# GpSimd's sum of the exponentials takes in key block 4, and the second queries' denominators are multiplied together one step later

## What is computed

```python
scores = jnp.einsum('bsnh,btnh->bnst', k, q) / math.sqrt(HEAD_SIZE)
ones = jnp.ones_like(scores)
scores = jnp.triu(scores) + -10000.0 * jnp.tril(ones, k=-1)
attn = jax.nn.softmax(scores, axis=2)
out = jnp.einsum('bnkq,bknh->bqnh', attn, v)
```

## Time and profile before

| | before |
|---|---|
| median of 3 runs | 1672.31 us (1671.54 to 1673.26) |
| profiled execution, its own time | 1674.67 us |
| its span, first to last instruction | 1672.8 us |
| PE busy | 1574.5 us, 94% of the span |
| DVE busy | 957.4 us, 57% |
| ACT busy | 742.1 us, 44% |
| POOL busy | 601.9 us, 36% |
| mean granted PE clock | 0.977 |

### The profile page before, as it was taken

The page is one execution under the profiler, slowest core; times in us unless marked ns, Lnnn a source line. Parts: engine busy times, 40 slices in busy tenths (PEclk is TensorE's granted clock), DMA queues, the critical chain, the costliest instruction groups (busy, mean ns, idle before and its releaser), DMA issues.

```text
span 1672.8 us, 24916 instructions
## 1 busy us (share of the span) xinstructions
PE 1574.5 (94%) x9630; PEld 671.1 (40%) x9632; DVE 957.4 (57%) x1784; ACT 742.1 (44%) x1206; POOL 601.9 (36%) x808
## 2 busy tenths in 40 slices
PE   5899999999999999999997699999999999999997
PEld 2334333443443434334432234444444444444443
DVE  5667766778766777667777333563534343434344
ACT  5346555566555665556655433232222222222221
POOL 4344654567456755655666630020000000000000
PEclk8899999999999999999988889999999999999998
DMA  5212111222220233012215631121101010101000
GB/s 183 90 50 52 50 28 51 66 73 80 79 61 24 79 85 95 25 40 79 85 47 159 213 109 45 52 100 32 51 26 51 25 51 26 51 25 51 0 26 26
DMA packets 59398, 106.25 MB, mean 64 GB/s; under 512 B 11408, under 2 KB 11408, under 8 KB 59024
## 3 DMA queue, kind: packets, MB, share of 16 engines
q1 hardware_dynamic: 59280, 104.66, 20.3%
HBM read 54.02 MB, written 25.17 MB: 47 GB/s over the span
## 4 chain that ended last, share of the span: by engine, by line
PE 70%; DVE 11%; POOL 8%; issue 4%; ACT 4%; DMA 1%; SPq 1%; DVEq 0%; ACTq 0%; POOLq 0%
PE ps L865 25%; PE ps L786 15%; PE ps L882 12%; PE ps L849 9%; DVE mcol L1105 6%; POOL pt L1311 4%; PE ps L823 4%; ACT pt L968 2%; PE ps L799 2%; PE ps L807 1%; DVE st L995 1%; PE ps L753 1%; POOL rs L1236 1%; SPq L665 1%; POOL pt L1302 1%
## 5 line engine op out<-in xcount | busy, mean ns | idle before, releaser
L968 ACT ACTIVATE pt<-ps,nrm 128x512 f32<-128x512 f32 (+1 forms) x640 | 362.1, 645 | 339.4 <-PE ps L823 310.2
L865 PE MATMUL ps<-x2in,gu 128*128 128x512 f16 x2048 | 463.9, 380 | 0.0
L1105 DVE TENSOR_REDUCE mcol<-ps 128x1 f32<-128x512 f32 (+3 forms) x768 | 369.5, 546 | 81.5 <-PE ps L807 53.8
L865 PEld LDWEIGHTS ps<-x2in,gu 128*128 128x128 f16 x2048 | 200.7, 98 | 240.8 <-issue 1.9
L1233 POOL TENSOR_SCALAR rs<-mv 128x1 f32<-128x1 f32 x120 | 24.9, 207 | 665.6 <-DVE mv L999 660.1
L1180 DVE SCALAR_TENSOR_TENSOR hf<-ps,usc,sg 128x512 f32<-128x512 f32 x128 | 96.1, 751 | 265.2 <-PE ps L865 252.6
L1311 POOL TENSOR_TENSOR pt<-pt 128x1024 f32<-128x1024 f32 x96 | 227.5, 2390 | 2.9 <-ACT pt L968 2.4
L984 ACT ACTIVATE hh<-hf 128x512 f16<-128x512 f32 x128 | 80.7, 631 | 261.7 <-DVE hf L1180 248.1
L882 PE MATMUL ps<-wd,hh 128*128 128x512 f16 x512 | 194.0, 379 | 0.0
L882 PE MATMUL ps<-wd,hl 128*128 128x512 f16 x512 | 194.0, 379 | 0.0
L823 PE MATMUL ps<-qpack,kpack 98*128 98x512 f16 (+3 forms) x768 | 169.2, 337 | 23.1 <-DVE mcol L1105 16.5
(11 more groups left out here) (116 smaller groups left out, 1618.0 us busy)
## 6 DMA issues: line engine op xcount, KB each, us to landing
qpack<-stage SPq DMA_DIRECT2D x192, 64.0 KB, 2.0
kpack<-stage SPq DMA_DIRECT2D x192, 64.0 KB, 2.0
xr<-in_x SPq DMA_DIRECT2D x32, 256.0 KB, 2.8
x1d<-xr SPq DMA_DIRECT2D x32, 256.0 KB, 2.4
x2d<-x2s SPq DMA_DIRECT2D x32, 256.0 KB, 2.0
x2in<-x2d SPq DMA_DIRECT2D x8, 1024.0 KB, 5.6
x1in<-x1d SPq DMA_DIRECT2D x8, 1024.0 KB, 5.8
out_x<-yy SPq DMA_DIRECT2D x32, 256.0 KB, 2.0
```

The lines of the kernel that those rows point to most:

```text
L865: mm = pe.matmul(bk, GU[:, c, m, i * 128:(i + 1) * 128], x2in[:, 1 - k, :, p, c, :], start=p == 0 and c == 0, stop=p == 1 and c == 3)
L968: act.activation(Pt[:, PBUF[step], h, off:512], ps[:, BANK[job], off:512], ACT.Exp, scale=esc).then_inc(s_ex, 1)
L1105: mm = dve.tensor_reduce(mcol[:, n % 2, col:col + 1], ps[:, BANK["max", n, i, h], at:at + w], AX.X, ALU.max)
```

## The change

POOL's sum takes in block 4 as well: two more additions of 128x1024 elements in step 8 of each group, the first ahead of the selects of block 5, the second behind them (in groups 14 and 15 both ahead). The den job of block 4 is gone. The den jobs of the sum and of block 5 leave step 9 and stand, with that of blocks 6 and 7, in step 0 of the next group, ahead of num. Bank 7 therefore stays in `RING` until step 0, where the sum's den job now opens the accumulation. Two waits come with it: the exponentials of block 6 wait for POOL's addition of block 4, which read the same buffer, and those of step 0 of the next group wait for block 5's den job. In groups 14 and 15 the den jobs of step 0 stand behind the scores of that step.

```diff
--- before.py
+++ after.py
@@ -150,12 +150,12 @@
 
     if step is None:
         return []
-    summed = step[1] == 1 and step[2] < 4
-    out = [] if summed else [("den",) + step]
+    of, j, kb = step
+    out = [("den", of, j, k) for k in ([kb] if j == 0 else [0, 5, 6] if last(j, kb) else [])]
     out.append(("num",) + step)
-    if summed and step[2] > 0:
-        out += [("sum",) + step + (h,) for h in (0, 2) if h == 0 or s != 7 or n >= NG - 2]
-    return out + [("den", n, 1, 0)] * (s == NS - 1)
+    if j == 1 and 0 < kb < 5:
+        out += [("sum",) + step + (h,) for h in (0, 2) if h == 0 or s not in (7, 8) or n >= NG - 2]
+    return out
 
 
 def order_of_jobs():
@@ -216,7 +216,7 @@
             plan += [("score", n, j, kb, h) for h in range(4)]
             if n < NG - 2 and pend is not None and last(*pend[1:]):
                 plan += [("invert",) + pend[:2], ("normalise",) + pend[:2]]
-            if s == 7 and n < NG - 2:
+            if s in (7, 8) and n < NG - 2:
                 add(("sum",) + pend + (2,))
             if s == NS - EARLY and n + 1 < NG:
                 plan += [("mjoin", n + 1), ("mturn", n + 1)]
@@ -237,7 +237,7 @@
             pend = (n, j, kb)
         if n + 2 < NG:
             add(("packs", n + 2))
-    plan += [("den",) + pend, ("num",) + pend, ("invert",) + pend[:2], ("normalise",) + pend[:2]]
+    plan += products_of(pend, NG, 0) + [("invert",) + pend[:2], ("normalise",) + pend[:2]]
     tail = [with_dev(job) for s in range(12) for job in rows.get(NS * NG + s, [])]
     started = max(job[1] for job in plan if job[0] == "woproj") + 1
     left = list(range(started, NT))
@@ -339,7 +339,7 @@
     elif kind == "step":
         if 5 in RING:
             RING.remove(5)
-        if 7 in RING and job[2] == 8:
+        if 7 in RING and job[2] == 0:
             RING.remove(7)
         if job[2] not in projections(job[1]) and FREE == [5]:
             RING.append(5)
@@ -350,7 +350,7 @@
             RING.append(7)
         continue
     elif kind == "den":
-        if job[2:] in ((0, 0), (1, 4)):
+        if job[3] == 0:
             FREE = [5]
             take(job, 7)
         continue
@@ -381,7 +381,8 @@
 
 
 
-SUMMED = [i for i, (j, kb) in enumerate(STEPS) if j == 1 and kb < 4]
+
+SUMMED = [i for i, (j, kb) in enumerate(STEPS) if j == 1 and kb < 5]
 PBUF, BEFORE, used_by = {}, {}, {}
 for step in range(1, NS * NG + 1):
     n, i = divmod(step - 1, NS)
@@ -829,10 +830,10 @@
                     ks = PBUF[STEP[a]]
                     if kind == "den":
                         e.wait_ge(s_const, 7)
-                        if kb == 4 * j:
+                        if kb == 0:
                             bank(job)
-                        if kb < 4 * j:
-                            e.wait_ge(s_sum, NO["sum", n, 1, 3, 2])
+                        if (j, kb) == (1, 0):
+                            e.wait_ge(s_sum, NO["sum", n, 1, 4, 2])
                     elif kb == 0 and (n, j) != (0, 0):
                         e.wait_ge(s_at, 2 * n + j)
                     elif kb == 0:
@@ -848,7 +849,7 @@
                             heads = ones[:] if kind == "den" else V[b % 2][:, kb_, g * 128 + 32 * h:g * 128 + 32 * h + 32]
                             mm = pe.matmul((DEN if kind == "den" else NUM)[rows, q0:512], heads,
                                            Pt[:, ks, h, at:at + 512 - q0],
-                                           start=kb_ == (4 * j if kind == "den" else 0),
+                                           start=kb_ == 0,
                                            stop=kb_ == 4 * j + 3)
                     mm.then_inc(s_den if kind == "den" else s_num, 1)
                 elif kind == "gate_up":
@@ -962,6 +963,8 @@
                         e.wait_ge(s_num, BEFORE[step])
                         if before[1] == SUMMED[0]:
                             e.wait_ge(s_den, NO["den", before[0], 1, 0])
+                        elif STEPS[before[1]] == (1, 5):
+                            e.wait_ge(s_den, NO["den", before[0], 1, 5])
                         elif before[1] in SUMMED:
                             e.wait_ge(s_sum, NO[("sum", before[0]) + STEPS[before[1]] + (h // 2 * 2,)])
                     e.wait_ge(s_sc, NO[job])
@@ -1306,6 +1309,8 @@
                     n, j, kb, h = a
                     e.wait_ge(s_num, STEP[n, 1, 0])
                     e.wait_ge(s_ex, NO["score", n, j, kb, h + 1])
+                    if kb == 4:
+                        e.wait_ge(s_dg, 2 * DIAG[n, j, kb] - (h == 0))
                     if kb > 1:
                         e.wait_ge(s_sum, NO["sum", n, j, kb - 1, h])
                     pool.tensor_tensor(Pt[:, 2, h:h + 2, :], Pt[:, 2, h:h + 2, :], Pt[:, PBUF[STEP[a[:3]]], h:h + 2, :],
```

## The result

The changed kernel takes 1685.58 us (median of 4 runs, 1684.48 to 1686.85) against 1672.09 us (4 runs) for the kernel before: a ratio of 1.0081, 95% interval 1.0066 to 1.0096. It is slower by 13.5 us. The forecast was 1670.8 us with a range of 1664.0 to 1677.5: the sign and the range were both wrong.

What follows compares the result with a forecast made beforehand. PE was taken to bound groups 0 to 13, while in groups 14 and 15 it already waits. The terms -2.4 + 1.9 - 1.0 = -1.5 us gave 1670.8 us, with a range of 1664.0 to 1677.5.

Steps and rivals of the forecast that it cites:

- the whole possible gain of the idea: Removing one den job per group, 0.88 us each on PE: 14.1 us in all, 12.3 in groups 0 to 13.
- The waits for the selects: Step 9: PE waits for block 5's selects, queued behind POOL's first addition; some 10 of 12.3 us come back.
- D - 0.88: Step 9: D is the old start of block 5's den; without a wait PE gets there 0.88 us sooner.
- The rule that was dismissed: GpSimd contends with VectorE for SBUF interfaces; conversions are hit (2.18 against 0.67 us), reductions of PSUM are not.
- The move, costed at nothing in groups 0 to 13: The den jobs of the sum and block 5 go from step 9 to the next step 0, at no cost.
- the small credit: Bank 7 in the ring for steps 8 and 9, and 1.5 us more for DVE in step 0: 1.0 us gained.
- The gain of group 13: Group 13 has no projection in step 9 and its selects wait for ACT: the full -0.88 us.
- Groups 14 and 15, forecast +1.9: Both additions stand ahead of block 5's selects: 1.5 us in group 14 and 0.4 in group 15.
- Rival (C): Slower through POOL in groups 14 and 15: 4.7 + 3 instead of 1.9, so +4.3 us; chance 0.18 together with (B).
- The hole of 3.20 us: Group 14: POOL's DMA wait behind the selects takes in 3.20 of the additions' 4.66 us, leaving 1.46.
- Rival (B): PE's clock halves behind new waits, 1.6 us lost at each place; four places give +4.9 us, 1677; chance 0.18 with (C).

Runs made afterwards that it cites:

- the run with the halves from PSUM: Changed kernel with the row maxima's two 16-bit halves made straight from PSUM by two DVE instructions in place of three: 1683.66 us, ratio 1.0063.
- the late order: Changed kernel with both additions behind block 5's selects and, in groups 0 to 13, PE's transposition of the row maxima behind step 8's projection: 1726.12 us.

## Why the prediction was wrong

**"That is the whole possible gain of the idea": 12.3 us in groups 0 to 13.** This term failed. The run without additions gives -3.3 us in groups 0 to 13, not -12.3. Taking the job away shortened the stretch it stood in by 13.2 us there, and 9.6 us of it came back as waits at the transposition, one step later. The row was right, 0.88 us from start to start; the step from there to the path wasn't. The text asked whether "PE then waits for what took its place" for POOL's selects alone. It never asked what DVE does while PE runs that job. The row that says so stood 2 us further on in the same timeline: join done at 580.87, transposition at 581.07. The slack was 0.2 us and the job 0.88. In eleven of the fourteen groups the join was also longer than by itself, beside POOL's old instructions, a price that the text didn't have either.

**The waits for the selects**, some 10 us in groups 0 to 12, were forecast as a sum of POOL's rows. Group 1: 3.55 forecast, 4.30 measured. Groups 4, 8 and 12: 1.31 forecast, 1.07 measured. In all the others, where 0.1 to 0.8 was forecast, there is none of over 0.06: PE came later than D - 0.88 because of the new wait at the transposition, so the two delays overlapped. The mechanism held, and the size was near where POOL was late by much.

**The rule that was dismissed.** The text said that the conversions are the ones hit by POOL's additions and "the reductions of PSUM in the other groups are not". That is true of the reductions: 681 ns after, 680 before. But DVE runs more than reductions in step 8. The cast, the difference and the join read and write SBUF, and no price was given for them beside an addition. The traces show them held to the end of it. The Trainium skill (SBUF — State Buffer, section "Who interferes with whom") has the rule in full: a VectorE instruction in a 2-port mode, or with two SBUF inputs while GpSimd's reads SBUF, and the GpSimd instruction exclude each other for the whole instruction, and whoever issues first wins. The trace agrees: a cast of 0.21 us took 2.31 us beside an addition of 2.35. So the first question of a change that puts 75 us on POOL is which DVE instructions with these operands lie in the same step. In groups 4, 8 and 12 this cost 0.88 us each; over the kernel 2 to 6 us.

**The move, costed at nothing in groups 0 to 13,** cost 4.4 us when made alone, but nearly nothing in the changed kernel: without the additions, step 9 of groups 0, 2 to 4, 6 to 8 and 10 to 12 is 1.50 us longer, which is what step 8 had lost in the move alone. Groups 5 and 9 pay 0.33 us more, and groups 0 and 1 0.8 and 1.6 in all. Against that, step 0 of groups 6 and 10 is 1.13 us shorter, as its waits of 0.61 us went: 2.3 us where the small credit was put at 1.0. The gain of group 13 was larger than forecast, 2.65 for 0.88 us.

**Groups 14 and 15, forecast +1.9, were +6.8 us** by the trace and +4.2 us as a change alone. Rival (C) was nearer: its bounds of 4.7 and 3 make 7.7. (With their order as before, the two groups took 101.2 to 103.9 us in six traces; with the change, 108.4 to 110.7 in four.) The hole of 3.20 us was taken to swallow most of the additions. In the changed kernel PE waits for the selects at once, as in groups 1, 4, 8 and 12 (in group 15, at 975.14, 9.45 us for the 8.02 before):

```profile
922.04 4.65 POOL L1316 TENSOR_TENSOR pt<-pt 128x1024 f32<-128x1024 f32 x2
926.65 1.42 POOL L1305 TENSOR_SCALAR_AFFINE_SELECT pt<-pt 128x256 f32<-128x256 f32 x2
...
928.13 1.51 PE L850 MATMUL ps<-pt,v 128*32 128x384 f32 x8 [2.71 <-POOL pt L1305]
...
975.14 1.93 PE L850 MATMUL ps<-pt,v 128*32 128x512 f32 x8 [9.45 <-POOL pt L1305]
980.48 1.51 PE L850 MATMUL ps<-pt,v 128*32 128x384 f32 x8 [2.01 <-POOL pt L1305]
```

The hole lay behind the selects, and PE's product waits for the selects themselves. How the 6.8 us divide between these waits, the held selects (1.42 for 0.78 us), the clock and later loads was not separated; the additions are 2.7 and 4.4 us of the two groups, and putting them behind the selects takes back 2.8 and 2.1 of it.

**Rival (B), the granted clock,** came true in group 1. Its step 9 took 9.71 us, where 6.41 before and the 1.50 that the move brings make 7.91: 1.8 us lost where 1.6 was put, most of it without the additions too (9.31 us). Groups 4, 8 and 12, with 1.07 us of waiting, kept 1.00 in the changed kernel's profile, but two of them did not in that of groups 0 to 13 alone, at 1.7 us each. In groups 14 and 15 the mean clock was 0.82 (860 to 989.6 us) for 0.85 before. So (B) holds in part, and how much it weighs in the median is open.

**Together**, in groups 0 to 13: removal and move bring -3.3 us instead of -12.3 and -1.0 of credits, and the additions cost 10.8 us for the 9.9 forecast (3.1 in group 1, 1.8 in each of 4, 8 and 12, 1.2 and 1.5 in 5 and 9, -0.5 in 13). Groups 14 and 15 add 6.8 for 1.9. The two terms that were wrong are the worth of the removed job, by 9 to 10 us, and the last two groups, by 5. The additions' sum came out near by luck, because waits that didn't come were replaced by group 1's clock and by the hold.

## What to carry to other kernels

A job on the bounding engine is worth its length only if nothing else ends a little later than it: before you book the gain, look at each other engine's last row ahead of the next point where the two meet, and read the slack. Before work goes to GpSimd, list the VectorE casts in SBUF and the sums of two SBUF operands in the same stretch; each can be held to the end of a GpSimd instruction, however small it is itself, and some may be held already. Whether that costs time is read at the next point where the bounding engine waits for them: here a cast of 1.59 instead of 0.21 us cost nothing in seven groups. Where the source is in PSUM anyway, reading it from there took the two instructions out of reach.

## What the hardware showed that was not expected

The hold doesn't depend on the size of the VectorE instruction: 32x128 elements took 0.21 to 0.28 us alone and 2.31 to 2.34 us beside a GpSimd addition of 2.35 us, and 1.25 us beside one of 1.26 us. Not every instruction with its input in SBUF is held: the layernorms' statistics (L995 of the kernel before) took 0.67 to 0.69 us beside an addition, as alone. It works the other way too: two selects took 1.44 us instead of 0.78 where a VectorE sum of 0.67 us fell in the first. In the run with the halves from PSUM that sum (587.89 to 588.56) fell on the start of POOL's addition instead, and the selects took 0.79 us and the addition 2.81 instead of 2.36. And it was already in the kernel before, where nobody had looked for it: the join of 128x16 elements takes 0.17 us alone and up to 1.6 us beside POOL.

```profile
L1112 DVE TENSOR_TENSOR mcol<-mcol 128x16 f32<-128x16 f32 x13 | 9.0, 694 | 0.0
```

(The same line, in the stretch of 113 to 860 us.) The wait of 4.30 us on PE was followed by 6.4 us at half the clock, that of 2.16 us in the run without additions and that of 3.36 us in the late order by 3.4 us each. Of six waits of 1.07 us in two profiles, two were followed by 3.4 us at half the clock and four were not.
